# One fused GNN, Mamba and expert layer on one core: B and C rows on ScalarE's queue, token blocks by plain SyncE DMA, larger clearing pieces, other PSUM banks, uneven adjacency shares

## What is computed

```python
a = relu(adj @ _layernorm(x) @ gcn_w + gcn_b)
h = (a - a.mean) * rsqrt(a.var + EPS) * ln_g + ln_b
xc, z = split(h @ w_in)                       # 256 channels each
u = silu(causal_conv4(xc) + conv_b)
low, B, C = split(u @ w_xp)                   # 8, 16 and 16 numbers for each token
dt = softplus(low @ w_dt + b_dt)
# for each of 16 states s and each of 256 channels, over the 8192 tokens in order:
#   hst[s] = exp(dt * A[s]) * hst[s] + dt * u * B[s];   y += hst[s] * C[s]
x = x + ((y + u * D_skip) * silu(z)) @ w_out
t = _layernorm(x)
H = gelu(t @ W1 + b1)                         # 512 numbers for each token
probs = softmax(H @ Wg + bg); e = argmax(probs)   # one of 8 experts for each token
x = x + probs[e] * (H @ Wd[e] + bd[e])
```

## Time and profile before

| | us |
|---|---|
| median of 3 runs | 1842.24 (1833.7 to 1849.21) |
| profiled execution | 1857.62 |
| its span, first to last instruction | 1855.8 |
| TensorE busy / VectorE busy | 1534.2 / 1535.7 |
| ScalarE busy / GpSimd busy | 877.1 / 874.5 |
| mean granted TensorE clock | 0.902 |

### The profile page before, as it was taken

One profiled execution on the slowest core, in us unless ns is written; L12 is line 12 of the kernel. 1 busy time (PEld: TensorE's weight loads), 2 busy tenths in 40 slices (PEclk: granted clock), 3 DMA queues, 4 the chain that ended last, 5 costly groups with the idle time before them and its releaser, 6 DMA issues. The chain is left out here.

```text
span 1855.8 us, 16772 instructions
## 1 busy us (share of the span) xinstructions
PE 1534.2 (83%) x4572; PEld 763.5 (41%) x4572; DVE 1535.7 (83%) x2015; ACT 877.1 (47%) x1558; POOL 874.5 (47%) x466
## 2 busy tenths in 40 slices
PE   6998888887989989898989888998989793633676
PEld 2433343333434545354544444443535341422444
DVE  8058898797899998989899989889999988898621
ACT  3134363452636464554646373646465554634311
POOL 0013333444345464645555554646464645557721
PEclk9999998999998999989999989899999996655788
DMA  8788999999897887879697868688787864333320
GB/s 306 252 299 308 307 337 306 338 317 324 305 329 264 307 294 262 282 255 317 246 322 257 311 233 309 248 307 286 283 299 266 309 215 170 101 124 136 120 70 12
DMA packets 164640, 479.42 MB, mean 258 GB/s; under 512 B 19780, under 2 KB 50512, under 8 KB 164418
## 3 DMA queue, kind: packets, MB, share of 16 engines
q1 hardware_dynamic: 155074, 453.31, 70.7%
q0 software_dynamic: 8320, 20.86, 3.5%
q10 hardware_dynamic: 1152, 4.19, 0.6%
HBM read 448.20 MB, written 33.22 MB: 259 GB/s over the span
## 5 line engine op out<-in xcount | busy, mean ns | idle before, releaser
L1162 PE MATMUL ps_adj<-ring,nodes 128*128 128x512 f32 x2048 | 957.6, 616 | 89.4 <-DMA ring<-adj 66.3
L496 POOL TENSOR_TENSOR h_c<-hidden,bc_ring 128x1024 f32<-128x1024 f32 x256 | 601.0, 2348 | 866.4 <-DVE inject L1030 603.2
L957 DVE TENSOR_TENSOR_SCAN hidden<-decay,state,inject 128x512 f32<-128x512 f32 x512 | 627.6, 1268 | 79.5 <-ACT decay L585 54.1
L1162 PEld LDWEIGHTS ps_adj<-ring,nodes 128*128 128x128 f32 x2048 | 397.0, 198 | 612.0 <-issue 480.2
L1030 DVE TENSOR_TENSOR inject<-dtu_sb,bc_ring 128x1024 f32<-128x1024 f32 x256 | 314.6, 1229 | 55.3 <-DMA bc_ring<-bc_dram 35.1
L585 ACT ACTIVATE decay<-dt_sb,negA 128x512 f32<-128x512 f32 x512 | 340.1, 714 | 8.8 <-DVE dt_sb L984 8.6
L1000 DVE TENSOR_TENSOR y_sum<-y_sum,h_c 128x1024 f32<-128x1024 f32 x224 | 273.8, 1222 | 23.9 <-POOL h_c L496 20.8
L578 ACT COPY state<-hidden 128x2 f32<-128x2 f32 x255 | 49.3, 193 | 473.3 <-DVE hidden L957 471.0
L460 POOL DMA_INDIRECT out<-o_sb,out_at x68 | 92.0, 1354 | 71.6 <-DVE o_sb L862 58.7
L455 POOL DMA_INDIRECT bins<-rec,dest x60 | 87.3, 1455 | 10.8 <-issue 10.2
L450 POOL DMA_INDIRECT got<-bins,row_at x60 | 85.0, 1416 | 14.6 <-issue 11.5
(11 more groups left out here) (201 smaller groups left out, 1387.0 us busy)
## 6 DMA issues: line engine op xcount, KB each, us to landing
ring<-adj SPq DMA_DIRECT2D x512, 512.0 KB
bc_ring<-bc_dram SPq DMA_DIRECT2D x256, 512.0 KB, 5.8
wd_ring<-wd_rows SPq DMA_DIRECT2D x64, 320.0 KB
bins<-nodes SPq DMA_DIRECT2D x128, 129.0 KB, 7.8
nodes<-x_rows ACTq DMA_DIRECT2D x8, 512.0 KB, 12.2
x_tile<-x_rows SPq DMA_DIRECT2D x16, 256.0 KB
wd_rows<-Wd SPq DMA_DIRECT2D x8, 256.0 KB
ring<-Wd SPq DMA_DIRECT2D x1, 2048.0 KB, 7.5
```

The costliest lines, as they stand in the source:

```text
L496: nc.gpsimd.tensor_tensor(h_c[:, s % 2], hidden[:, s % 2], over_halves(bc_ring[:, s % BC_RING, 1]), ALU.mult).then_inc(hc_ready, 1)
L957: scan = nc.vector.tensor_tensor_scan(hidden[:, s % 2, h], decay[:, s % 2, h], inject[:, h], state[:, h, s:s + 1], ALU.mult, ALU.add)
L1162: last = nc.tensor.matmul(ps_adj[:, 0], nodes[:, m], ring[:, g % RING, m % GROUP], start=(m == 0), stop=(m == J - 1))
```

## The change

Five edits come together.

- **B and C rows.** All of their DMAs, to DRAM and back, are issued by ScalarE (`fetch_rows`). At the end of its slot s it issues the row of state s+2, after a wait for the `h_c` product of state s-2. Before, SyncE issued it for state s+1 in its own slot s.
- **Blocks.** GpSimd's gathers are gone. SyncE loads the first record number of a block into a register and reads 128 records with a step of 8 by a plain DMA (`load_rows`). It does this in slot 7, after the waits that GpSimd had in slot 6 (the scatters of tile i-2 among them), ahead of the experts' weights. In the flush the same, and `control` has 17 steps: an absent record is marked in `absent` and sorted out in `finish`.
- **Clearing.** 32 DMAs of 516 KB (128 pieces of 4128 bytes) instead of 128 of 129 KB (128 pieces of 1032 bytes), spread evenly over the 48 slots of stages 1 to 3.
- **Banks.** H goes to `ps_e` 0, `ps_e` 1, `ps_y` and `ps_f` 1. Only the last of the four waits for `ps_f`, dbc waits for no gelu, the first dt product waits for the gelu of `ps_f` 1, which comes first of the four, after all four H products.
- **Shares.** From stage 4 on, the 32 adjacency pieces of a tile lie in the slots by SHARE.

```diff
+EVEN = (2,) * SLOTS
+SHARE = (3, 3, 2, 3, 2, 2, 2, 1, 2, 2, 0, 3, 2, 3, 0, 2)
-                counts = table.get(i, () if table is LEAD else (2,) * SLOTS)
+                counts = table.get(i, () if table is LEAD else SHARE)
...
-            return (ps_f[:, 0], ps_f[:, 1], ps_y[:, 0], ps_e[:, 0])[k]
+            return (ps_e[:, 0], ps_e[:, 1], ps_y[:, 0], ps_f[:, 1])[k]
...
             def clear_bins(n):
-                sp.dma_start(bins.ap()[n * P:(n + 1) * P], nodes[:].rearrange("p j d -> p (j d)")[:, 0:REC]
-                             ).then_inc(zero_in[n * AREAS // FILLS], 16)
+                area, part = n // PARTS, n % PARTS
+                size = SPACE // AREAS
+                width = size * REC // P // PARTS
+                cells_of = bins.ap()[area * size:(area + 1) * size].rearrange("(p n) c -> p (n c)", p=P)
+                sp.dma_start(cells_of[:, part * width:(part + 1) * width],
+                             nodes[:].rearrange("p j d -> p (j d)")[:, 0:width]).then_inc(zero_in[area], 16)
+
+            def load_rows(dst, slot, done):
+                for j in range(PICKS):
+                    first = sp.value_load(row_at[0:1, slot, j:j + 1], min_val=0, max_val=SPACE - EXPERTS * (P - 1) - 1)
+                    sp.dma_start(dst[:, j], bins.ap()[bass.ds(first, P, EXPERTS)]).then_inc(done, 16)
...
                     if s == 7 and batch:
                         sp.wait_ge(table_in, 16 * 2 * EXPERTS)
+                        for n in range(AREAS):
+                            sp.wait_ge(zero_in[n], 16 * PARTS)
+                        c.wait(ctrl_step, -4, 13)
+                        c.wait(scat_in, -2, 16 * BLOCKS)
+                        c.wait(o_ready, -6, PICKS + 1)
+                        load_rows(got[:, p], p, row_in[p])
                         c.wait(by_done, -6, PICKS)
-                        c.wait(ctrl_step, -4, 13)
                         load_experts(wd_ring[:, p], p, wd_in[p])
-                    for d, t in next_state(s, mamba, front):
-                        freed = c.value(hc_ready, d, t - BC_RING + 1)
...
+                    if s == 13 and i == TILES - 1:
+                        c.wait(scat_in, -1, 16 * BLOCKS)
+                        late_rows(0)
+                        late_experts(0, -2)
...
         @block.gpsimd
-                    if batch and s == 6:
...
-                        c.wait(scat_in, -2, 16 * BLOCKS)
-                        c.wait(o_ready, -6, PICKS + 1)
...
-                    if batch and s in (6, 7):
-                        for j in (2 * (s - 6), 2 * (s - 6) + 1):
-                            gather_rows(got[:, p], p, j, row_in[p])
...
         @block.scalar
+                def fetch_rows(s):
+                    for d, t in ((0, s + 2), (1, s + 2 - SLOTS)):
+                        if (mamba if d == 0 else front) and 0 <= t < SLOTS:
+                            if t == 0:
+                                c.wait(rows_out, d, 16)
+                            c.wait(hc_ready, d, t - BC_RING + 1)
+                            act.dma_start(bc_ring[:, t % BC_RING],
+                                          bc_dram.ap()[p if d == 0 else q, t:t + 1].broadcast_to([P, 2, T])
+                                          ).then_inc(bc_in[t % BC_RING], 16)
...
                     if ffn and s == (5 if fast else 8):
-                        for k in range(4):
-                            c.wait(h_done, -1, k + 1)
+                        c.wait(h_done, -1, 4)
+                        for k in (3, 0, 1, 2):
...
+                        c.wait(rows_ready, 1, 1)
+                        act.dma_start(bc_dram.ap()[q].rearrange("s h n -> h s n"), rows_sb[:]).then_inc(rows_out, 16)
...
                         exp_decay(s)
+                    fetch_rows(s)
...
         @block.tensor
                     if ffn and s == 7:
                         c.wait(xt_ready, -1, 1)
-                        c.wait(xz_ready, 1 if front else 0, 4 if front else 0)
                         c.wait(bh_ready, -5, 4)
+                        c.wait(o_ready, -5, PICKS + 1)
                         for k in range(4):
+                            if k == 3:
+                                c.wait(xz_ready, 1 if front else 0, 4 if front else 0)
...
                     if front and s == f[8]:
                         c.wait(u_ready, 1, 1)
-                        if ffn:
-                            c.wait(h_ready, -1, 1)
...
                         if ffn:
-                            c.wait(h_ready, -1, 2)
+                            c.wait(h_ready, -1, 1)
```

More of the change, by code:

```diff
@@ L371, in body @@
                 q = 1 - p
-                f = FRONT.get(i, range(SLOTS))
                 if i == TILES - 2:
@@ L387, in body @@
                     if i in (1, 2, 3):
-                        for n in range(3 * (SLOTS * (i - 1) + s), min(3 * (SLOTS * (i - 1) + s + 1), FILLS)):
+                        k = SLOTS * (i - 1) + s
+                        for n in range(AREAS * PARTS * k // (3 * SLOTS), AREAS * PARTS * (k + 1) // (3 * SLOTS)):
                             clear_bins(n)
@@ L416, in body, with late_rows, late_experts @@
                         dma.then_inc(x_in, 16)
-            bodies(sp, body)
-            for f in range(FLUSH):
-                k = BATCHES + f
-                if f != 2:
-                    Count(sp, k).wait(by_done, -2 if f < 2 else -3, PICKS)
-                sp.wait_ge(flush_step, 20 * f + 20)
-                load_experts(experts_of(f), 2 + f, wd_late_in[f])
+            def late_rows(f):
+                sp.wait_ge(flush_step, 17 * f + 17)
+                load_rows(rows_of(f), 2 + f, row_late[f])
+            def late_experts(f, d):
+                if d is not None:
+                    Count(sp, BATCHES + f).wait(by_done, d, PICKS)
+                load_experts(experts_of(f), 2 + f, wd_late_in[f])
+            bodies(sp, body)
+            late_rows(1)
+            late_rows(2)
+            late_experts(1, -2)
+            late_experts(2, None)
+            late_rows(3)
+            late_experts(3, -3)
+            sp.wait_ge(o_ready, (BATCHES + 1) * (PICKS + 1))
+            late_rows(4)
+            late_experts(4, -3)
             sp.wait_ge(sum_step, 1 + 9 * BLOCKS)
@@ L437, in _ @@
             constant(lane[:], [[0, 1]], 0, 1)
-            constant(lane8[:], [[0, 1]], 0, EXPERTS)
             constant(need[:], [[0, 1]], EXPERTS, EXPERTS)
@@ L445, in _ @@
                 constant(id_col[:, q], [[P, BLOCKS]], q * T - 2 * T, 1)
-            pool.wait_ge(start_v, 1)
-            constant(got[0:1, 0, 0, REC - 1:REC], [[0, 1]], 1 << 30, 0)
-            def gather_rows(dst, slot, j, done):
-                nc.gpsimd.indirect_dma_start(
-                    out=dst[:, j], out_offset=None, in_=bins.ap(),
-                    in_offset=bass.IndirectOffsetOnAxis(ap=row_at[:, slot, j:j + 1], axis=0)).then_inc(done, 16)
             def scatter_rows(q, b):
@@ L476, in body @@
                         c.wait(id_step, -2, 1)
-                    if batch and s == 6:
-                        pool.wait_ge(last_in, 16)
-                        for n in range(AREAS):
-                            pool.wait_ge(zero_in[n], 16 * FILLS // AREAS)
-                        c.wait(ctrl_step, -4, 13)
-                        c.wait(scat_in, -2, 16 * BLOCKS)
-                        c.wait(o_ready, -6, PICKS + 1)
                     if fast and s == 10:
@@ L487, in body @@
                         c.wait(id_step, -1, 1)
-                    if fast and s == 13:
-                        c.wait(scat_in, -1, 16 * BLOCKS)
-                        pool.wait_ge(flush_step, 20)
                     if mamba:
```

78 lines of the change are left out of this document (24 added, 54 removed).

## The result

| | before | after |
|---|---|---|
| median of 20 runs, in turn on one chip | 1846.26 us | 1855.84 us |
| range | 1829.02 to 1854.39 | 1842.05 to 1867.74 |
| ratio | | 1.0056, 95% interval 1.0034 to 1.0078 |
| profiled execution / its span | 1857.62 / 1855.8 | 1855.66 / 1853.9 |
| mean granted TensorE clock | 0.902 | 0.891 |

The change makes the kernel slower by 0.56%. That is little, but the whole interval lies above 1. The forecast was 1822, against a median of 1842.24 for before.

The account below looks back on a forecast made before the run. VectorE's own order was taken to pace the recurrence, with transfers the limit in stages 1 to 3. Terms -6 -12 +10 -5 -7 = -20 us, from the median 1842.2 to 1822 us; range 1780 to 1870.

Parts of the forecast that it names:

- rival B: Slot 8 of stages 4 to 13: SyncE's stop behind the scatter wait starves TensorE; kernel at 1860 us, chance 0.24.
- Stages 1 to 3: Transfers are the limit there; larger clearing pieces gain and moved rows give nothing: -12 us, bounds -18 and +5.
- Stage 0: VectorE's 12.2 us of row waits shrink as rows pass adjacency pieces on ScalarE's queue; TensorE gives part back: -6 us.
- Stage 14: Rows no longer stand behind dense weights on SyncE and the gelu wait is gone, against slot 13's late row: -5 us.
- Stage 15 and flush: Waits behind gathers before the last y_sum and for the flush's residual product both go: -7 us, bounds -10 and +8.
- Rows on ScalarE's queue: Stages 4 to 13: slot 13's row, issued behind slot 11's gelus, comes late; its wait replaces the decay wait.
- The landing below 5.8 us: A row on ScalarE's queue no longer stands behind all earlier adjacency pieces, so it would land in under 5.8 us.
- Banks and shares: Stages 4 to 13: dbc stops waiting for a gelu, up to 3.8 us per stage; two adjacency pieces move to earlier slots.
- Blocks by SyncE: Stages 4 to 13: y_sum waits of 1.4 us per stage end; SyncE's slot 7 stop leaves gelus at -0.5 or 3.5 us later.
- The term for stages 4 to 13: Banks, shares, blocks by SyncE and rows by ScalarE together: +1.0 us per stage, +10 in all, bounds -3 and +7 per stage.
- the landing of 3.5 us: Slot 8's first adjacency piece, issued about 1281, lands in 3.5 us as with free engines, not 5.8 behind other pieces.
- the turns between queues: Each DMA engine alternates between queues with work, so rows on ScalarE's queue would not wait behind all earlier adjacency pieces.

## Why the prediction was wrong

The sign was wrong: forecast 20 us faster, measured 10 slower (0.56% of 1846.26), inside the range, near the rival B (1860). B had the place and the cause right, SyncE's stop starving TensorE in slot 8. But it priced the loss at slot 13 (+4.8 us per stage), where the waits did not grow (36.5 and 35.4 us), so that its number came close is in part luck. Step by step:

*Stages 1 to 3*, -12 foreseen, -16.7 seen, and -15.1 from the clearing alone. Right, a little small. The rows did nothing there, as the prediction had it.

*Stage 0*, -6 foreseen, -0.3 seen: mis-sized. VectorE's wait for rows fell from 12.2 us to 3.2, and its wait for ScalarE's decay rose from 2.7 to 11.8.

*Stage 14*, -5, seen -4.9: VectorE's waits there fell from 3.9 for rows and 4.4 for decay to 3.2 and 1.3. *Stage 15 and flush*, -7, seen -4.0 and, against the 108 us of the flushes with before's code, about -4. Right in size; no experiment has these parts alone.

*Rows on ScalarE's queue*, right: the wait at slot 13 moved from decay to the row. The landing below 5.8 us, which a second queue might have given, did not come: the page's median for `bc_ring` is 5.9 on ScalarE's queue (before with the rows alone moved) and 6.0 on SyncE's (before with the larger clearing), so a queue of its own gave the rows no faster landing.

*Banks and shares*, right in kind: 38 us of gelu waits gone, and 13 and 21 us longer stages when each is undone.

*Blocks by SyncE*, the step that failed. The term for stages 4 to 13 was +10 and measured +43. The working carried SyncE's stop to slot 13 alone, and left out that dbc itself becomes late and with it the decay of slot 10. Three things in it:

1. "I take -0.5, since a stop of 12 us on SyncE surely empties its queue": the landing of 3.5 us. The queue was empty of pieces and full of experts' weights, which the working had counted only as issue time. The piece landed after 6.6 us. This was hidden in part, because the issue came 3.7 us sooner than foreseen (45.0, against 1281 - 1232.3 = 48.7): the scatters had landed early enough for the first block load to go out at 36.7, while the working let the wait last to 39.4 (1271.67). So TensorE resumed at 51.5, not 50.7.
2. "From there it has the two pieces of slot 8 before dbc, but none in slot 10, so the batch's products come as long after this point as they now come after 1283.42." That was 17.2 us; it is 20.6 (1295.20 to 1315.83). 3.1 of the 3.4 are the two pieces at the clock that fell while TensorE stood (6.73 for 3.60; over the ten stages 5.7 for 3.5, by the table, so 2.2 us each). The fall of the clock had no place in the sum.
3. The path by slot 10 was not seen. The prediction followed the lateness only through the batch's gelus to slot 13. But dbc, behind two pieces, came 6.7 us later into the stage (57.2 against 50.5), ScalarE stood on it, and the decay of slot 10 cost VectorE 45.6 us over ten stages. Its note that SyncE's stop delays "all adjacency pieces of slot 8 and later" had the means for it: behind dbc on ScalarE stand the copy of B and C and then that decay.

An estimate from these numbers says what each is worth. In stage 11 of the change the scan of slot 10 starts 4.6 us after dbc (1306.36 - 1301.77). With the prediction's own resuming at 50.7 and two pieces at full clock (3.5), that scan would start at 50.7 + 3.5 + 4.6 = 58.8, 0.6 later than before's 58.2: a small loss by this path. The fallen clock adds 2.2 and the later resuming 0.8, and the sum is the 61.8 measured. That is 3.6 of the 4.3 us by which a stage is longer.

What would have shown it right or wrong was named well: stages of 103 and more with TensorE starved after slot 7 mean B. The choice between B and the forecast hung on two or three microseconds per stage, and I gave the forecast 0.42 and B 0.24 on the strength of one landing time taken from a stretch with free DMA engines.

On the landing, the Trainium skill (DMA: Bandwidth & Descriptors, "Queues, rings and completion order") has a rule that bears on it: a transfer's semaphore update is a strongly ordered write, which comes only after every earlier write of that DMA engine, over all its queues. The runs agree with it: weights on the same queue ahead of a piece, 6.6 to 7.6 us in place of 3.7 to 3.9; a row on the other queue ahead of it, 5.7 in place of 3.7. Transfers that merely share the same engines' time would also land later, and no run here tells the two apart. The prediction took from the same section only the turns between queues.

The change as a whole pays with the stop placed well: with the experts' loads in slot 9 it is 3.6% faster than before and (0.9645 / 1.0056) 4.1% faster than the change as made.

## What to carry to other kernels

When a wait moves onto the engine that issues the transfers, list every issue behind it, and count each twice: once as issue time, once as bytes ahead of the first transfer that someone needs. Put the needed transfers first: the same stop cost 7 us less per stage behind the pieces of the next two slots than ahead of them. And follow a late product through every in-order engine that reads it; the first one to stand on it (here ScalarE's copy of B and C) hands the delay on to work that has nothing to do with it.

A row of the page can name a wait that disappears without gain: 36.5 us of decay waits became 27.0 us of row waits when the rows went to ScalarE's queue; and when the rows were issued earlier, row waits fell from 35.3 to 6.3 us, while decay waits rose from 7.9 to 51.7 and TensorE's for pieces from 57.2 to 76.9.

## What the runs showed of the hardware that was not expected

- A transfer on one queue delays the landing of a transfer that another queue issues 1.6 us later: 5.7 us in place of 3.7 for a 512 KB piece behind a 512 KB row.
- Rows of 512 KB landed after much the same time from either queue: 5.9 us (median of the page) from ScalarE's, with before's rows moved there, and 6.0 from SyncE's, with before's larger clearing pieces.
- After 11.1 us of standing TensorE's clock was 0.50, and eight products took 6.73 us in place of 3.60; after 3.6 us of standing, with the experts in slot 9, the eight still took 5.29. In two of the ten stages of that kernel the clock stayed at 1.00 after stops of 3.1 and 2.4 us, and TensorE reached dbc in 3.5 us. Over the ten stages of the change the fallen clock is 2.2 us per stage by itself.
- The last scatter of a stage landed 3.9 and 4.0 us after its issue where SyncE put nothing beside it, and 7.0 us after it beside the experts' weights (7.2 beside adjacency pieces, with blocks and experts in slot 9).
